# Adding gated expert outputs on VectorE in the second layer, and writing out the wide stages' loops

## The reference

```python
x = x + _L1_conv_ref(_ln_c(x), ...)
t = _to_tokens(x)
t = t + _L1_ffn_ref(_ln_t(t), ...)
...
# experts of the second layer, on every token xt:
weights = top_p / top_p.sum(axis=-1, keepdims=True)
h = gelu(einsum('end,edh->enh', xe, W1) + b1[:, None, :])
y = einsum('enh,ehd->end', h, W2) + b2[:, None, :]
out = (weights[:, :, None] * sel).sum(axis=1)
...
# experts of the third and fourth layer:
h = jax.nn.silu(h1) * h3
y = jnp.einsum('neh,ech->nec', h, w2)
out = jnp.einsum('ne,nec->nc', gates, y)
```

## Time and profile before

| | |
|---|---|
| median of 3 runs | 2269.54 us (2264.92 to 2270.61) |
| the profiled execution | 2262.46 us, its span 2260.6 us |
| TensorE busy | 1582.5 us (70%) |
| VectorE busy | 1702.9 us (75%) |
| ScalarE busy | 1361.3 us (60%) |
| GpSimd busy | 998.4 us (44%) |
| granted TensorE clock, mean | 0.822 |

### The profile page before, as it was taken

How to read it: one execution, slowest core, us unless ns; L and a number is a source line. 1 busy time by engine, 2 the same in 40 slices (tenths; PEclk the granted TensorE clock), 3 DMA queues, 4 the chain that set the end, 5 groups by cost and what they waited for, 6 DMA issues and landing times.

```text
span 2260.6 us, 51407 instructions
## 1 busy us (share of the span) xinstructions
PE 1582.5 (70%) x16820; PEld 1182.9 (52%) x16821; DVE 1702.9 (75%) x2874; ACT 1361.3 (60%) x2473; POOL 998.4 (44%) x955
## 2 busy tenths in 40 slices
PE   4467777778677667766776933699923599958994
PEld 3334434435343334335776832588822488847884
DVE  3567777876877668646788977788887788849886
ACT  0256665686779676876565840377741377747774
POOL 1024334432223212783232567344478477754443
PEclk8578768787887677998887975699965699979997
DMA  7000000000001100000000110010021111120002
GB/s 309 0 26 1 1 26 1 1 1 1 1 1 68 58 1 1 18 21 23 16 20 16 31 58 22 22 28 27 24 106 46 26 37 37 34 66 25 27 28 90
DMA packets 53032, 76.29 MB, mean 34 GB/s; under 512 B 14905, under 2 KB 37642, under 8 KB 50206
## 3 DMA queue, kind: packets, MB, share of 16 engines
q1 hardware_dynamic: 30658, 43.26, 6.1%
q0 software_dynamic: 22208, 30.81, 3.9%
HBM read 40.89 MB, written 35.19 MB: 34 GB/s over the span
## 4 chain that ended last, share of the span: by engine, by line
PE 24%; DVE 16%; POOL 10%; issue 8%; ACT 2%; DMA 1%; POOLq 0%; SPq 0%; DVEq 0%; ACTq 0%
PE bank L1640 8%; PE bank L1641 7%; POOL rows L588 5%; PE bank L1654 4%; POOL y L612 3%; DVE tmp L1089 2%; PE bank L1656 2%; DVE hl L1254 2%; PE bank L1394 1%; POOL x L626 1%; DVE act L1250 1%; PE bank L1536 1%; PE bank L1626 1%; DVE st L913 1%; DVE tmp L1066 1%
## 5 line engine op out<-in xcount | busy, mean ns | idle before, releaser
L612 POOL DMA_INDIRECT y<-ysb,ids x352 | 396.2, 1126 | 474.2 <-DVE ysb L1240 402.3
L626 POOL TENSOR_TENSOR x<-x,ysb 128x256 f32<-128x256 f32 x288 | 267.8, 930 | 658.6 <-DVE ysb L1328 650.0
L778 ACT ACTIVATE hb<-bank,bias_sb 128x512 f32<-128x512 f32 x432 | 299.5, 693 | 238.6 <-issue 137.4
L588 POOL DMA_INDIRECT rows<-rowsb,pos x288 | 322.4, 1120 | 98.5 <-issue 74.8
L1250 DVE TENSOR_TENSOR act<-bank,act 114x512 f32<-114x512 f32 x352 | 241.2, 686 | 132.8 <-ACT act L796 85.3
L796 ACT ACTIVATE act<-bank 114x512 f32<-114x512 f32 x352 | 210.2, 597 | 185.0 <-PE bank L1641 181.8
L1640 PE MATMUL bank<-xT,gA 128*114 128x256 f16 x1056 | 298.6, 307 | 18.2 <-issue 9.4
L1640 PE MATMUL bank<-xT,uA 128*114 128x256 f16 x1056 | 272.3, 282 | 28.0 <-DVE act L1250 21.6
L1641 PE MATMUL bank<-xT,gB 128*114 128x256 f16 x1056 | 279.9, 282 | 0.0
L1641 PE MATMUL bank<-xT,uB 128*114 128x256 f16 x1056 | 273.8, 283 | 0.0
L1654 PE MATMUL bank<-dW,hl 114*128 x2112 | 260.7, 224 | 6.3 <-DVE hl L1254 5.2
(11 more groups left out here) (246 smaller groups left out, 3390.5 us busy)
## 6 DMA issues: line engine op xcount, KB each, us to landing
xs<-rows SPq DMA_DIRECT2D x176, 65.0 KB
stage<-up SPq DMA_DIRECT2D x8, 1368.0 KB, 8.2
rows<-land POOLq DMA_DIRECT2D x8, 1137.5 KB, 17.7
y<-ysb,ids POOLq DMA_INDIRECT x352
rows<-rowsb,pos POOLq DMA_INDIRECT x288
stage<-down SPq DMA_DIRECT2D x2, 1368.0 KB
rowsb<-y SPq DMA_DIRECT2D x4, 640.0 KB, 6.4
rows<-land POOLq DMA_DIRECT2D x4, 585.0 KB, 20.4
```

Of the source, the lines that this page charges most:

```text
L588: pool.indirect_dma_start(rows_d[l - SPARSE][h], bass.IndirectOffsetOnAxis(pos[h][:, k, j:j + 1], 0), words(h)[:, j * RW // 2:(j + 1) * RW ...
L612: pool.indirect_dma_start(y_d[h], bass.IndirectOffsetOnAxis(ids[h][:, t * SUB + u:t * SUB + u + 1], 0), ysb[t % UNROLL][:, u * C:(u + 1) * ...
L626: pool.tensor_tensor(xv, xv, tg[u % 2], ALU.add).then_inc(s["added"], 1)
L778: ins = a.activation(dst[:, 0:SPAN * P], PB[w % 3][:, :], ACT.Gelu, scale=1.0 / WSCALE, bias=b1T[l][:, at:at + 1])
```

## The change

In the whole second layer VectorE adds a unit's gated result to x itself: four instructions of 128 x 64, one for each token tile, each of which reads the result from PSUM, multiplies it by the tile's gate (one value per partition) and adds x. They replace VectorE's one multiplication of 128 x 256 and GpSimd's addition. GpSimd keeps the adds of the first layer, and after them goes straight to scatter(2, 0). TensorE's wait for a free bank is moved from "gated" to "added" there. And middle() is gone: the nine bodies of every wide stage are written out on TensorE, VectorE and ScalarE. SyncE's loop of loads stays.

```diff
+        def direct(l, h, u):
+            return l == 1
...
-        def middle(eng, body):
-            with eng.Fori(1, LOOPS - 1) as i:
-                body(i)
...
-            def dense(l, h, aside, begin):
+            def dense(l, h):
...
                     pool.tensor_tensor(xv, xv, tg[u % 2], ALU.add).then_inc(s["added"], 1)
-                    if u >= begin:
-                        next(aside, None)
-                        next(aside, None)
-
-            placed = weave(1, 1).index(next(k for k in weave(1, 1) if k >= ROUTE + 20)) // 2 + 4
+
             first = scatter(SPARSE, 0)
-            for l in range(SPARSE):
-                for h in range(HALVES):
-                    dense(l, h, first, placed if (l, h) == (1, 1) else NUNIT)
+            for h in range(HALVES):
+                dense(0, h)
             for _ in first:
                 pass
...
-                if aside is None:
-                    middle(v, body23)
-                else:
-                    for i in range(1, LOOPS - 1):
-                        body23(i)
+                for i in range(1, LOOPS - 1):
+                    body23(i)
...
                     v.wait_ge(s["down_ps"], vb + k + 1)
+                    if direct(l, h, u):
+                        v.wait_ge(s["added"], ub + u)
+                        for t_ in range(SPAN):
+                            xt = x[h][:, s8 * SPAN + t_, :]
+                            ins = v.scalar_tensor_tensor(xt, PB[3 + (ub + u) % 3][:, t_ * C:(t_ + 1) * C],
+                                                         gd[h][:, s8 * SPAN + t_, e:e + 1], xt, ALU.mult, ALU.add)
+                        ins.then_inc(s["added"], 1)
+                        return
...
-                        wait_from(pe, s["gated"], ub + u - 2)
+                        wait_from(pe, s["added" if ub + u - 3 >= unit_base(1, 0) else "gated"], ub + u - 2)
...
-                    pe.wait_ge(s["gated"], unit_base(SPARSE, 0))
+                    pe.wait_ge(s["added"], unit_base(SPARSE, 0))
```

More of the change, by code:

```diff
@@ L836, in moe @@
                 body(0, first=True)
-                if aside is None:
-                    middle(a, body)
-                else:
-                    for i in range(1, LOOPS - 1):
-                        body(i)
+                for i in range(1, LOOPS - 1):
+                    body(i)
                 body(LOOPS - 1, last=True)
```

## The result

The changed kernel takes **2214.39 us**, median of 4 runs (2213.12 to 2219.39), the kernel before 2270.07 (2264.92 to 2272.9, 4 runs). The ratio is 0.9761, with a 95% interval of 0.9738 to 0.9785. That is 55.7 us less. Forecast were 2237 us with a range of 2216 to 2260: faster, as said, but the gain is 22 us larger and lies outside the range. The profiled execution took 2215.43 us, its span is 2213.6 us.

What follows compares the result with a forecast made beforehand. No single engine: VectorE mostly in the woven dense part, GpSimd's adds and sends in the bare part, GpSimd's queue in moe(3, 0). Terms -30.6 + 16 - 10.0 - 7.8 = -32.4 us gave a 2237 us median, range 2216 to 2260.

Steps and rivals of the forecast that it cites:

- term 1: Second layer's bare part: without GpSimd's adds, units come every 2.40 us and moe(2, 0) starts 30.6 us earlier.
- term 2: Second layer's woven part: VectorE's new additions, half of 32.5 us on the path, cost +16 us, between 0 and 33.
- term 3: moe(2, 1) written out: nine bodies at 17.54 instead of 18.65 us, 10.0 us less.
- term 5: moe(3, 1) written out on TensorE and ScalarE: seven bodies gain 1.11 us each, 7.8 us less.
- Term 4: moe(3, 0) written out: GpSimd's queue sets its end, sooner tiles wait for a buffer: 0, perhaps up to 3 us.
- Rival D: Dense part: the four new instructions do not overlap, VectorE becomes the bound, slower at 2284 us; chance 0.10.
- the sign that I had named: In moe(3, 0): GpSimd still never waits, and VectorE waits for its buffers instead.
- B: Woven part absorbs VectorE's extra work, so that cost is 0: 2221 us; chance 0.17.
- C: All of VectorE's extra work in the woven part lies on the path, +33 us: 2254 us; chance 0.15.
- E: Wide stages: written-out loops save nothing because longer programs must be brought in, 2255 us; chance 0.08.

Runs made afterwards that it cites:

- e1: Changed kernel's direct additions and GpSimd order, but with the loops of the kernel before in moe(2,1), moe(3,0) and moe(3,1); 2241.15 us, ratio 0.9882.
- e3: Changed kernel with moe(3,0) alone as a loop again on TensorE, VectorE and ScalarE; 2224.16 us, ratio 0.9808.
- e10: e3 with VectorE's low-part subtraction in moe(3,0) reading its second operand from a stale PSUM bank, low parts not computed; 2212.77 us, ratio 0.9749.
- e11: Changed kernel once more, unchanged, beside e9 on the same chip; 2213.17 us, ratio 0.9764.
- e5: Changed kernel with 9 instead of 4 sends of the last table ahead of moe(3,0)'s first y write; 2210.56 us, ratio 0.9732.
- e2: Kernel before with only the three loops written out on TensorE, VectorE and ScalarE; 2241.82 us, ratio 0.9879.
- e4: Changed kernel with VectorE's direct additions only from unit 28 of dense(1,1) on, GpSimd adding before that; 2205.32 us, ratio 0.9731.
- e9: Changed kernel with the edits of e4 and e5 together; 2201.77 us, ratio 0.9700.

## Why the prediction was wrong in size

The direction held, and so did the mechanism of terms 1, 2, 3 and 5. Term 4 failed in its reasoning, and term 2 in its size. Each can be set against its stage.

1. **Bare part, -30.6 us; measured -34.4.** "I take 2.40 us, between ScalarE's 2.32 and the 2.46": it was 2.31, ScalarE's own. Nothing of GpSimd's adds was left to disturb VectorE, so there was no reason to stay above the bound: 39 x 0.09 = 3.5 us. The table was forecast to be ready just in time and was some 3 us early: 72 sends took 97.7 us, not 103.2, and the last unit starts moe(2, 0).

2. **VectorE's new work, +16 us; measured +7.5** (+7.8 to +8.1 in e1, e3, e10 and e11, +10 in e5). Two sizes were off. The instructions occupy 0.193 us, not 0.21, so the net is 0.43 - 0.18 = +0.25 us a unit and not 0.325: 25 us of VectorE's time, not 32.5. And the path took 30% of it, not half. The stretch of the subtraction did go, as the term had it; the groups by form of the changed kernel from 515 to 903 us (790 and 761 ns before):

```profile
L1318 DVE SCALAR_TENSOR_TENSOR x<-bank,land,x 128x64 f32<-128x64 f32 x372 | 79.5, 276 | 10.8 <-PE bank L1592 10.3
L1307 DVE TENSOR_TENSOR act<-hb,act 128x512 f16<-128x512 f32 x93 | 64.0, 688 | 19.8 <-ACT act L772 19.4
L1307 DVE TENSOR_TENSOR hl<-hb,hl 128x512 f16<-128x512 f32 x92 | 63.2, 687 | 27.1 <-ACT hl L772 26.3
```

For the new instruction's price the estimate by the Trainium skill, "VectorE: DVE Perf Modes", The TRN2 errata, was the closer one: 4 x 0.192 = 0.77 us against my 0.84, and 0.77 was measured. For the instruction that it replaces it was not: 0.392 us against 0.34 measured. So for the difference its +0.375 and my +0.50 lie on either side of the measured +0.43. Of the 0.07 us that I added for the value per partition, from one 576-wide line, 0.193 - 0.145 = 0.05 came; whether that value costs it, no run tells. Rival D (the four don't overlap) fell on the same number: one lasts 276 ns, the next starts after 193.

3. **moe(2, 1), -10.0 us; measured -8.9** (-9.1 to -10.2 in e2 to e5). Right.

4. **moe(3, 0), 0; measured -9.0. This is the step that failed.** The premise, "GpSimd's queue sets its end", was right (e3, e5). The conclusion, "tiles that come sooner wait for a buffer", was not, because it took GpSimd's instruction times as given. They depend on what VectorE runs at their start: 1.19 us on the two-operand subtraction, 0.98 otherwise (e10). VectorE's waits for its buffers, the sign that I had named, hardly grew: 7.9 us in this stage before, 8.7 after. The trace of before had the means, 1109 ns for the writes and 1082 for the sends:

```profile
L612 POOL DMA_INDIRECT y<-ysb,ids x86 | 95.4, 1109 | 33.0 <-issue 25.6 <-DVE ysb L1240 7.4
L588 POOL DMA_INDIRECT rows<-rowsb,pos x67 | 72.5, 1082 | 20.4 <-issue 19.8 <-POOL rowsb L596 0.6
```

while half of the 72 sends of another stage took 962 ns or less. I saw the possibility ("if GpSimd's instructions got shorter") and sized it at 3 us with no row for it. An upper bound was to be had from these: 153 x (1.10 - 0.97) = 20 us.

5. **moe(3, 1), -7.8; measured -8.1.** Right.

On the stages from layer 1 on, -32.4 were forecast and -52.5 came: 3.8 of the difference is term 1, 8.5 term 2, 9.0 term 4, less 1.1 for term 3. The last 3 us up to the medians' 55.7 are within the interval of the ratio. The shift of 7 us from the profiled execution to the median was applied rightly; most of it fits the short layer 0 of that one execution.

Of the rivals, B (woven part free) came nearest in time, 2221 us, but is not what happened: VectorE's work cost 7.5 us there, and e4's stage gets it back. That its time came near is luck: its term 2 was 7.5 us too low and term 4, which it shares with the forecast, 9.0 too high. C, D and E are out. What the range lacked was an error of two terms in the same direction. It left room for each alone.

## What to carry to other kernels

A queue that bounds a stage is not a constant. Where GpSimd issues indirect DMAs back to back, compare its mean instruction with the shortest one; if they differ, find what the other engines run at its start, VectorE with two SBUF operands among them. A changed pace elsewhere moves that overlap.

Where an engine's work is partly hidden, the share on the path is not a fixed number: it was 30% for the first 25 us here and 54% for the next 51. Move work only in the part of a stage where the receiving engine has room; the same edit won 34 us in the bare part and lost 7.5 in the woven one.

Compare executions by stages between marks, never by absolute times: 5.5 us of the shift lay in code that nobody changed. A stage of a single execution can still mislead: the same woven part took 406.8 us in e4 and 414.7 in e9.

## What the hardware showed that was not expected

- In moe(3, 0) a GpSimd indirect DMA takes 0.98 us beside the rest of VectorE's work and 1.19 when it starts with the subtraction, which has two SBUF operands (means over 142 in the kernel before). With the second operand in PSUM it is 0.98 again (e10). Beside longer instructions of VectorE with two SBUF operands it is longer still: in scatter(2, 1) of the kernel before, 12 sends that start in L1089 (0.82 us) take 1.36 in the mean, and 7 that start in the layer norm's L915 and L934 (1.2 to 1.5 us) take 1.60.
- The body of four tiles costs 18.65 us as a hardware loop and 17.6 written out, in layers 2 and 3 alike where nothing is woven in. The longer program, rival E's reason, showed no price. What in the loop costs the 1.05 us, no run tells.
- Four 128x64 instructions from PSUM with a value per partition occupy 0.77 us, eight of 128x32 1.28: the split in halves costs 0.51 us for the same elements.
